# A fused attention and graph-attention kernel: another order of mask, term transposes and second normalisation, and another split of the last six batches

## The reference, cut to what matters

```python
# layer 0: 6 heads of 64
q, k, v = heads(x @ Wq + bq), heads(x @ Wk + bk), heads(x @ Wv + bv)
probs = softmax(q @ k.T / 8 + where(adj, 0, NEG))
x = layernorm(x + (probs @ v) @ Wf + bf)
# layer 1: 12 heads of 32
h = einsum('bnd,ade->bane', x, W);  th = tanh(h)
attn = th @ w_src + (th @ w_dst).T            # (12, 128, 128) for each batch
attn = softmax(where(adj, leaky_relu(attn, 0.2), -999))
f = elu(attn @ h + b)
gate = sigmoid(x @ H_w.T + H_b)
x = layernorm(x + gate * f + (1 - gate) * x)
```

## Time and profile before

| | us |
|---|---|
| median of 3 runs | 1118.89 (1118.72 to 1119.07) |
| the profiled execution | 1119.08 |
| its span, from the first to the last instruction | 1117.3 |
| PE busy | 1053.9 (94%) |
| VectorE busy | 888.8 (80%) |
| ScalarE busy | 882.6 (79%) |
| GpSimd busy | 766.3 (69%) |

### The profile page before, as it was taken

How to read it: one execution, slowest core, us unless ns; L and a number is a source line. 1 busy time by engine, 2 the same in 40 slices (tenths; PEclk the granted TensorE clock), 3 DMA queues, 4 the chain that set the end, 5 groups by cost and what they waited for, 6 DMA issues and landing times.

```text
span 1117.3 us, 25374 instructions
## 1 busy us (share of the span) xinstructions
PE 1053.9 (94%) x8300; PEld 881.2 (79%) x8300; DVE 888.8 (80%) x1826; ACT 882.6 (79%) x3255; POOL 766.3 (69%) x911
## 2 busy tenths in 40 slices
PE   5889999999999999999999999999999999997773
PEld 5678888888888888888888888888888888886652
DVE  5457878888887888888788888878888887888875
ACT  3348888888888888888888888888888888888864
POOL 1467776776777677677767767776776777667652
PEclk9999999999999999999999999999999999999986
DMA  9101010020101002010100201010020101000000
GB/s 273 57 2 57 16 64 24 8 72 16 65 16 57 31 8 72 16 65 16 58 30 9 72 16 65 15 54 33 9 72 16 64 16 44 16 8 16 16 15 22
DMA packets 25892, 44.65 MB, mean 40 GB/s; under 512 B 2462, under 2 KB 23714, under 8 KB 25762
## 3 DMA queue, kind: packets, MB, share of 16 engines
q1 hardware_dynamic: 23234, 41.91, 11.0%
q10 hardware_dynamic: 2496, 1.12, 0.5%
q0 software_dynamic: 32, 0.00, 0.0%
HBM read 30.43 MB, written 12.58 MB: 39 GB/s over the span
## 4 chain that ended last, share of the span: by engine, by line
PE 57%; POOL 26%; issue 9%; DVE 5%; ACT 2%; DMA 1%; POOLq 0%; ACTq 0%; DVEq 0%
PE ps_b L253 13%; PE ps_d L253 13%; POOL z L963 9%; PE ps_a L253 7%; PE ps_d L460 5%; POOL xT_lo L911 5%; PE ps_a L382 4%; PE ps_s L362 3%; POOL p L990 3%; PE ps_s L354 2%; POOL s L955 2%; PE ps_c L470 2%; POOL thw L998 2%; POOL y L957 2%; PE ps_d L448 1%
## 5 line engine op out<-in xcount | busy, mean ns | idle before, releaser
L584 ACT ACTIVATE z<-z,s 128x128 f32<-128x128 f32 x768 | 297.3, 392 | 6.3 <-DVE s L791 6.3
L963 POOL TENSOR_TENSOR z<-z,mask 128x512 f32<-128x512 f32 x192 | 218.4, 1166 | 0.4 <-ACT z L678 0.4
L584 ACT ACTIVATION_READ_ACCUMULATOR z<-z,s 128x1 f32 x768 | 146.7, 191 | 0.0
L611 ACT ACTIVATE p<-ps_s,s 128x128 f32<-128x128 f32 x384 | 134.7, 378 | 11.4 <-DVE s L769 11.4
L990 POOL TENSOR_TENSOR p<-p,s 128x768 f32<-128x768 f32 x64 | 94.2, 1471 | 57.2 <-DVE s L797 57.2
L460 PE MATMUL ps_d<-ident,z 128*128 128x128 f32 x768 | 118.4, 277 | 10.5 <-ACT z L584 9.7
L952 POOL TENSOR_SCALAR s<-s 128x1 f32<-128x1 f32 x128 | 28.8, 225 | 141.5 <-DVE s L890 129.9
L998 POOL TENSOR_TENSOR thw<-th,w_sd 128x768 f32<-128x768 f32 x64 | 117.5, 1836 | 2.8 <-ACT th L634 2.8
L678 ACT ACTIVATE z<-ps_d 128x512 f32<-128x512 f32 x192 | 100.8, 598 | 20.9 <-PE ps_d L448 20.9
L460 PEld LDWEIGHTS ps_d<-ident,z 128*128 128x128 f32 x768 | 90.6, 142 | 18.2 <-ACT z L584 10.5
L791 DVE TENSOR_REDUCE s<-z 128x8 f32<-128x1024 f32 x64 | 77.9, 1216 | 26.4 <-POOL z L963 25.8
(11 more groups left out here) (156 smaller groups left out, 3398.0 us busy)
## 6 DMA issues: line engine op xcount, KB each, us to landing
x_cols<-in_xT_dram SPq DMA_DIRECT2D x16, 768.0 KB, 6.2
xb<-in_x_dram SPq DMA_DIRECT2D x16, 768.0 KB, 4.8
out_dram<-y SPq DMA_DIRECT2D x64, 192.0 KB, 1.9
z<-in_L_gnn_Wq_dram SPq DMA_DIRECT2D x1, 576.0 KB, 6.5
p1T<-in_L_gnn_Wk_dram SPq DMA_DIRECT2D x1, 576.0 KB, 8.8
qT<-in_L_gnn_Wv_dram SPq DMA_DIRECT2D x1, 576.0 KB, 11.2
kT<-in_L_gnn_Wf_dram SPq DMA_DIRECT2D x1, 576.0 KB, 13.3
z<-in_L_gnn_W_dram SPq DMA_DIRECT2D x1, 576.0 KB, 11.9
```

The source lines that it names most:

```text
L584: done = act.activation(z[:, a, :], z[:, a, :], ACT.Exp, bias=neg1[:, a:a + 1], accum_out=sum1[:, a:a + 1])
L611: last = act.activation(p0[:, o, i, :], ps_s[:, o, i * N:(i + 1) * N], ACT.Exp, bias=neg0[:, k:k + 1], accum_out=sum0[:, k:k + 1])
L963: pool.tensor_tensor(z[:, 4 * q:4 * q + 4, :], z[:, 4 * q:4 * q + 4, :], mask[:, t, :].unsqueeze(1).broadcast_to([P, 4, N]), ALU.add).then ...
```

## The change

It has these parts.

- PE's order in every step: `scores_mask` goes from behind `logits` to ahead of `project_out`; `turn_sd` and the third `turn_p1` now follow chunk 0 of `project_out` and not chunk 1.
- GpSimd's order in every step: `second_norm` of a batch goes from the end of a step to the middle of the next one, behind the product of th and ahead of `first_norm`. `r1` and `mv1` are doubled for it.
- The last six batches (58 to 63, `UNFILLED` = 58): PE adds the mask to the logits by three more matmuls of the identity with the mask, `z_mask` of GpSimd is left out, ScalarE's exponentials don't accumulate, and VectorE sums them with three reductions, one ahead of its `p1T` copy and two behind `cols_R`.
- The products with v of the last two batches go from step j = 3 of iteration 15 to the steps j = 0 and 1 of iteration 16, ahead of `project_h`. ScalarE evacuates both; before it was ScalarE for one and VectorE for the other.

```diff
+UNFILLED = G * (NG - 1) - LAG
...
-        r1 = sb("r1", [P, D])
+        r1 = sb("r1", [P, 2, D])
...
             def fill_b(g, n, j):
+                if j == 3 and n + 1 == NG:
+                    return
...
+            def late_v(j):
+
+                pe.wait_ge(S["ctx_lo"], G * (NG - 1) + j)
+                if j == 0:
+                    pe.wait_ge(S["v_even"], 2 * NG - 1)
+                project_v(2 + j, ps_a)
...
-                    last = pe.matmul(heads, rows_L[tile, :], cols_R[tile, :, :], start=True, stop=True)
-                    last.then_inc(S["logits_ready"], 1)
+                    last = pe.matmul(heads, rows_L[tile, :], cols_R[tile, :, :], start=True, stop=(t < UNFILLED))
+                    if t < UNFILLED:
+                        last.then_inc(S["logits_ready"], 1)
+                if t >= UNFILLED:
+                    for q in range(3):
+                        pe.matmul(ps_d[:, q, :].rearrange("p (a n) -> p a n", a=4), ident_b[:],
+                                  mask[:, t, :].unsqueeze(1).broadcast_to([P, 4, N]), start=False, stop=True
+                                  ).then_inc(S["logits_ready"], 1)
...
+                    if n == NG and j < 2:
+                        late_v(j)
                     if gat:
                         project_h(tl, n, j)
...
-                    if att:
-                        project_out(ta, g, j, n, (0, 1))
-                    if gat:
-                        turn_sd(tl)
-                    if tail:
-                        turn_p1(tl - 1, gat, (2,))
-                    if att:
-                        project_out(ta, g, j, n, (2,))
-                    if gat:
-                        logits(tl)
                     if 0 <= ta and ta + 1 < B:
                         scores_mask(ta + 1)
+                    if att:
+                        project_out(ta, g, j, n, (0,))
+                    if gat:
+                        turn_sd(tl)
+                    if tail:
+                        turn_p1(tl - 1, gat, (2,))
+                    if att:
+                        project_out(ta, g, j, n, (1, 2))
+                    if gat:
+                        logits(tl)
                     if tail:
                         apply_p1(tl - 1, (j + 1) % 2, gat)
...
+                        if t < UNFILLED:
+                            done = act.activation(z[:, a, :], z[:, a, :], ACT.Exp, bias=neg1[:, a:a + 1],
+                                                  accum_out=sum1[:, a:a + 1])
+                        else:
+                            done = act.activation(z[:, a, :], z[:, a, :], ACT.Exp, bias=neg1[:, a:a + 1])
...
+                            if tl - 1 >= UNFILLED:
+                                act.wait_ge(S["sum1_ready"], 3 * (tl - 1 - UNFILLED) + q + 1)
...
+                def sum_exponentials(t, q):
+
+                    dve.wait_ge(S["exp1_ready"], 3 * t + q + 1)
+                    if q == 0:
+                        dve.wait_ge(S["inv1_ready"], t)
+                    dve.tensor_reduce(sum1[:, 4 * q:4 * q + 4], z[:, 4 * q:4 * q + 4, :], AX_X, ALU.add
+                                      ).then_inc(S["sum1_ready"], 1)
...
+                    if tail and tt >= UNFILLED:
+                        sum_exponentials(tt, 0)
                     if tail:
                         turned_p1(tt, 0)
...
+                    if tail and tt >= UNFILLED:
+                        sum_exponentials(tt, 1)
+                        sum_exponentials(tt, 2)
...
             def z_mask(t):
 
+                if t >= UNFILLED:
+                    return
+
...
+                    if has_tail(n, j, 3):
+                        second_norm(tl - 3)
                     if 0 <= ta - 1 < B:
                         first_norm(ta - 1)
...
-                    if has_tail(n, j, 2):
-                        second_norm(tl - 2)
             pipeline(pool, iteration)
+            second_norm(B - 1)
```

More of the change, by code:

```diff
@@ L123, in build_program @@
         inv1, sum1 = s2[:, 0:12], s2[:, 40:52]
[L124 removed]
+        st1, mv1, ve1, rs1, nm1 = s2[:, 16:22], (s2[:, 24:26], s2[:, 26:28]), s2[:, 28:29], s2[:, 30:31], s2[:, 32:33]
         fT = sb("fT", [P, C, N])
@@ L136, in build_program @@
         bf_in = th[:]
-        hb_row = r1[0:1, :]
+        hb_row = r1[0:1, 0, :]
         hb_rest = y[0:1, :, :]
@@ L365, in context @@
             def context(t, g, par, j, n):
-                if j == 0:
+                if j == 0 and n < NG:
                     pe.wait_ge(S["v_even"], 2 * g)
@@ L372, in context @@
                     else:
-                        pe.wait_ge(S["v_even"], 2 * g + 2)
+                        pe.wait_ge(S["v_even"], 2 * g + (1 if n + 1 == NG else 2))
                 else:
-                    if due(t):
-                        pe.wait_ge(S["ctx_lo"], t)
+                    if j == 0:
+                        pe.wait_ge(S["v_odd"], 2 * NG - 1)
+                    if j < 2:
+                        pe.wait_ge(S["late_v"], j + 1)
+                    pe.wait_ge(S["ctx_lo"], t)
                 pe.wait_ge(S["p0T_even"], t + 1)
@@ L391, in project_out @@
                         else:
-                            pe.wait_ge(S["v_odd"], 2 * g + 2)
+                            pe.wait_ge(S["v_odd"], 2 * g + (1 if n + 1 == NG else 2))
                     elif due(t):
@@ L515, in iteration @@
                         project_gate((2,))
+                    if 0 <= ta and ta + 1 < B:
+                        scores_mask(ta + 1)
                     if att:
-                        project_out(ta, g, j, n, (0, 1))
+                        project_out(ta, g, j, n, (0,))
                     if gat:
@@ L522, in iteration @@
                     if att:
-                        project_out(ta, g, j, n, (2,))
+                        project_out(ta, g, j, n, (1, 2))
                     if gat:
                         logits(tl)
-                    if 0 <= ta and ta + 1 < B:
-                        scores_mask(ta + 1)
                     if tail:
@@ L621, in iteration @@
                         evacuate_v(0)
+                    if n == NG and j < 2:
+                        act.wait_ge(S["v_made"], G * (NG - 1) + j + 3)
+                        act.activation(v[:, 1 - par, 2 + j, :], ps_a[:, 0:D], ACT.Copy).then_inc(S["late_v"], 1)
                     if qkv and n + 1 < NG and j == 3:
@@ L636, in iteration @@
                         exp1(tl - 1, 0, 4)
-                    if qkv and j == 3:
+                    if qkv and j == 3 and n + 1 < NG:
                         evacuate_v(2)
@@ L776, in iteration @@
                         t2 = tl - 2
-                        dve.wait_ge(S["exp1_ready"], 3 * (t2 + 1))
+                        if t2 < UNFILLED:
+                            dve.wait_ge(S["exp1_ready"], 3 * (t2 + 1))
+                        else:
+                            dve.wait_ge(S["sum1_ready"], 3 * (t2 + 1 - UNFILLED))
                         dve.reciprocal(inv1, sum1).then_inc(S["inv1_ready"], 1)
@@ L786, in iteration @@
                     if tail:
-                        dve.wait_ge(S["zm_ready"], 3 * tt + 2)
+                        if tt < UNFILLED:
+                            dve.wait_ge(S["zm_ready"], 3 * tt + 2)
+                        else:
+                            dve.wait_ge(S["z_ready"], 3 * tt + 2)
                         if due(tt):
@@ L798, in iteration @@
                     if tail:
-                        dve.wait_ge(S["zm_ready"], 3 * (tt + 1))
+                        if tt < UNFILLED:
+                            dve.wait_ge(S["zm_ready"], 3 * (tt + 1))
+                        else:
+                            dve.wait_ge(S["z_ready"], 3 * (tt + 1))
                         dve.tensor_reduce(neg1[:, 8:12], z[:, 8:12, :], AX_X, ALU.max, negate=True
@@ L813, in iteration @@
                         dve.wait_ge(S["tail_small"], 3 * t2 + 2)
-                        if due(t2):
-                            dve.wait_ge(S["y_ready"], t2)
-                        dve.scalar_tensor_tensor(r1[:], gate[:, t2 % 3, :], 1.0, ps_r, ALU.add, ALU.mult
+                        if due(t2 - 1):
+                            dve.wait_ge(S["y_ready"], t2 - 1)
+                        dve.scalar_tensor_tensor(r1[:, t2 % 2, :], gate[:, t2 % 3, :], 1.0, ps_r, ALU.add, ALU.mult
                                                  ).then_inc(S["tail_small"], 1)
@@ L844, in iteration @@
                         evacuate_k(2)
-                    elif qkv:
+                    elif qkv and n + 1 < NG:
                         evacuate_v(3)
@@ L885, in iteration @@
                         dve.wait_ge(S["tail_small"], 3 * t2 + 3)
-                        dve.scalar_tensor_tensor(r1[:], r1[:], 0.25, x1_, ALU.mult, ALU.add).then_inc(S["r1_ready"], 1)
+                        dve.scalar_tensor_tensor(r1[:, t2 % 2, :], r1[:, t2 % 2, :], 0.25, x1_, ALU.mult, ALU.add).then_inc(S["r1_ready"], 1)
```

(6 more changed lines are left out.)

9 lines of the change are left out of this document (3 added, 6 removed).

## The result

The changed kernel takes 1122.07 us (median of 20 runs, 1120.69 to 1125.13) against 1119.82 of the kernel before in the same comparison (20 runs, 1116.71 to 1124.42): a ratio of 1.0025, with a 95% interval of 1.0015 to 1.0034. By that ratio it is slower by about 2.8 us (by the medians 2.3), at the edge of the 0.2% that the prediction named as the least that can be told from none; it had the kernel 0.5 us faster. The profiled execution took 1123.46, its span is 1121.7.

A forecast was written before the change was run, and what follows sets the result against it. Bound by PE and its waits up to iteration 15, by the chain through all engines in the drain. -6.2 + 6.8 - 1.1 = -0.5 us gave 1118.6, 1118.4 as median; range 1111 to 1127.

The forecast's parts named there:

- The wait for p0: PE's wait for GpSimd's p0 in step j = 0 goes whole once y moves: 14 x 0.44 = -6.2 us.
- PE's new order: PE, each step: 0.33 - 0.07 - 0.14 = +0.12 us, in 57 steps +6.8 us (+1.1 to +16.5).
- The -0.14: PE behind the logits, each step: without the mask turn_f starts 2.42 and not 2.56 after them, waiting for fT.
- Costed at nothing: GpSimd's first_norm and xT_lo behind the moved y come up to 2 us later, into idle time: no cost.
- a sign of being wrong: turn_sd waiting for sd3_ready, since it comes 0.2 us earlier, would show the prediction wrong.
- The drain, -1.1: Last six batches and drain: -1.1 + 0.1 + 0.5 + 1.3 + 0.5 - 0.4 - 2.0 = -1.1 us (-3 to +1.5).
- The products with v: Moved out of iteration 15: of 3.1 us only -1.1 can be had; in iteration 16 they cost nothing.
- rival 5: VectorE bounds the drain, its sums finding no idle time: 1124 us; chance 0.07.
- the terms for the last batch: End of the drain: L791 starts about 0.9 us earlier without z_mask, exponentials give 1.1: -2.0 us.
- 4: Rival, slower: the mask ahead costs its waits too and the gap stays, +0.29 a step, 1128 us; chance 0.29.
- Rival 3: PE keeps all it saves if ScalarE has fT in time: a step loses 0.35 us, 1092 us; chance 0.08.

The follow-up runs named there:

- e11_y_gap: The changed kernel with second_norm (y) between z_mask and the scaling of p0 on GpSimd: 1.0002 of the kernel before.
- e2_norm: The kernel before with the second normalisation moved alone, nothing else of the change: 0.9921 of the kernel before.
- e1_order: The kernel before with TensorE's new order alone (mask ahead of the output projection, turn_sd behind its first chunk): 1.0060 of the kernel before.
- e9_x_first: The changed kernel with first_norm ahead of second_norm on GpSimd, both still behind thw: 1.0023 of the kernel before.
- e10_turns: The changed kernel with turn_x1 ahead of turn_f on PE: 1098.4 us, 0.9807 of the kernel before.
- e3_rest: The changed kernel with TensorE's order of before in the steps, all else of the change kept: 0.9933 of the kernel before.
- e5_mask_ahead: The kernel before with only the mask's two matmuls moved ahead of the output projection, turn_sd left in place: 1.0115 of the kernel before.
- e14_all: The changed kernel with turn_x1 ahead of turn_f, second_norm between z_mask and p0's scaling, and UNFILLED = B: 0.9857 of the kernel before.

## Why the prediction was wrong, step by step

**The wait for p0 goes whole: right, the term too small.** -6.2 was 14 times the matmuls' wait. The step j = 0 lost 0.53 instead of 0.44, where the weights are now loaded ahead as well, and j = 1 lost 0.06. In the stretch it is -7.3 instead of 12 x 0.44 = -5.3.

**PE's new order costs +0.12 a step: this is the step that failed.** Its parts nearly held. In e11_y_gap, against e2_norm, the way from the gate's bias product to the logits is longer by 0.27 (forecast +0.26), and behind the logits 0.13 is given back (forecast 0.14). From `turn_x1` to `turn_p0` another +0.03 appears, which the sum didn't have and whose cause is open. That makes 0.17 by these medians and 0.19 by the stretch (9.3 in 50 steps), with the overlap on sd taken out. The changed kernel pays 0.22: 11.2 in 50 steps above e2_norm, 12.8 in 57, where the sum had 6.8.

The -0.14 hides how much the order itself saves. From the logits to `apply_p1` it is 0.32 now and was 0.90 (medians), 0.58 less, of which the two mask matmuls that left are 0.33. The other 0.25 went with one change of the array's shape fewer, where the prediction had read 0.1 off a change; what it consists of wasn't taken apart. All of it but 0.13 was lost again in the wait for `fT`, as the prediction said.

**"Costed at nothing" for what stands behind the moved y: wrong.** I asked whether x1 and `xT_lo` would come too late, and found idle time ahead of them. I didn't ask what runs on VectorE at the time to which they move. `first_norm`'s last operation fell on the split of sd, L916 took 0.36 instead of 0.18 in the mean, and with `turn_sd` moved ahead PE waited: 1.2 to 1.9 us in the stretch. Neither edit does that alone: e2_norm has the slow subtraction with PE not there yet (12 waits, 2.2 us), e1_order has PE early and the subtraction fast. I had written this wait down as a sign of being wrong, but only because `turn_sd` comes earlier, and left it out of the sum and out of the range's reasons.

The Trainium skill, page "SBUF — State Buffer", section "SBUF: two separate sides", says that a VectorE operation with two SBUF inputs and a GpSimd operation that reads SBUF exclude each other: the one that starts first keeps their shared ports for its whole instruction, and the other waits. The traces agree for L916: all 35 slow ones of the changed kernel end 0.03 behind `first_norm`'s last operation, and all 35 of e9_x_first end 0.03 behind y's. What happens close to the start of GpSimd's operation is in the last section.

**The terms were added as if each stood alone.** In e1_order the stall at j = 0 also hid the new order's cost in one step of four. Taking it away and lengthening the step aren't independent: 4.9 us more than the sum in the stretch, of which, as an estimate, 12 x (0.44 - 0.18) = 3.1 is this cover and 1.2 to 1.9 the overlap on sd. The prediction counted 57 paying steps, so this cover is no error of its sum; it is why e1_order came out at the forecast 6.8, by luck, while a step that isn't covered costs 0.15 to 0.17.

**The drain, -1.1: the sum about right, its reasons half wrong.** From batch 58 to the end the profile has -1.3. The products with v gave -1.06 (forecast -1.1). Three steps took 15.25 to 15.27 instead of 14.9 (forecast 15.4), but from the masks on PE, not from VectorE's sums, so rival 5 fell. From the last `turn_p0` to the end 1.6 us were saved where 1.9 was forecast, which is within what that part varies by: it takes 55.2 in e9_x_first, 57.1 in the changed kernel and 58.4 in e11_y_gap, at mean granted clocks of 0.90, 0.83 and 0.77, and took 58.7 at 0.77 before. What the terms for the last batch are worth isn't shown.

The rivals: 4 came nearest, with a step over its limit of 0.17, but its +0.29 a step and its 1128 us were too much: the gap did shrink, and the wait that came on top was another than it named. Rival 3 asked for `fT` in time. e10_turns gives that in another way, by covering it: a step is then 0.14 to 0.20 shorter than with the old order, not 0.35.

In the stretch the parts add up as follows: forecast 50 x 0.12 - 12 x 0.44 = +6.0 - 5.3 = +0.7, measured +3.9. The order is 3.3 above its term, the overlap adds 1.9 and the normalisation takes off 2.0. These are differences of single traces, each good to some 0.7, so the order's own cost is the larger error and the overlap the smaller one.

## What to carry to other kernels

When a step moves on one engine, look at what every other engine does at the time to which it and all behind it move, not only whether there is idle time for it: here 0.7 us of GpSimd slowed a VectorE instruction of 0.18 us whose result TensorE had just been made to take earlier. Work that stood between a result and its use was paying for itself as cover; whoever moves it needs other work of that length. Here two groups of transposes in exchanged order turned a loss of 0.25% into a gain of 1.9%. Price two edits together where one removes a stall that hides the other's cost.

## What the runs showed of the hardware that was not expected

The granted clock falls in the drain in some executions, for part of a step (the clock of the column before the DMA share). The step to batch 60, of the changed kernel and of e9_x_first, which do the same work there:

```profile
1003.84:1018.75 14.91, 12.98 (x116) 11.07 (x116) 12.54 (x28) 12.36 (x49) 10.05 (x14) 1.00 0.04 14
```

```profile
1001.75:1018.21 16.46, 14.54 (x116) 12.32 (x116) 12.74 (x28) 12.46 (x49) 9.99 (x14) 0.90 0.04 13
```

A mean of 0.90 means 1.2 GHz instead of 2.4 for a fifth of the step, and costs 1.55 us. It happened in one step in the profiled executions of e3_rest, e9_x_first, e11_y_gap and e10_turns (0.89 there, and a step of 15.65), in three in e5_mask_ahead (16.74 to 16.77) and in e14_all, and in none in the other eight, the changed kernel among them. PE is busy 12 to 13 of 15 us there, in the middle of the program nearly always, where the clock stayed at 1.00. Time and mean clock go together over whole executions too: the twelve of e11_y_gap go from 1116.4 us at 0.995 to 1124.0 at 0.983. That is why differences of 2 us between single executions say little about an edit here.

A cast of one operand can be held by GpSimd too: half of the L914 take 0.37 in e10_turns, where they start 0.34 to 0.36 behind the start of L1008, and end 0.03 behind its end. In the row of e9_x_first above it takes 0.18, started 0.06 behind. The traces show where the line lies. Of the subtractions and casts of the split of sd that start while the last operation of a normalisation is under way, all that start up to 0.14 us behind its start in the profile run freely (0.17 to 0.22 us), and all that start later are held until 0.03 behind its end, but for a few first casts (L909) that start in its last 0.02 us. In the changed kernel the last free one starts 0.134 behind and the first held one 0.146; in e9_x_first 0.137 and 0.145. So which of the two comes first isn't decided by their starts in the profile as they stand, but some 0.14 us later on GpSimd's side or earlier on VectorE's; the traces don't say which.
